# Four neighbouring tokens per partition, with strided transposes and products, in an attention-and-experts kernel

## The reference

```python
x = x + layernorm(attn(layernorm(x), W_in, b_in, W_out, b_out, decay, mix))
x = x + layernorm(ffn(layernorm(x), gate_kernel, w0, w1, wo))
```

## Time and profile before

| | us |
|---|---|
| median of 3 runs (lowest to highest) | 312.19 (311.73 to 312.6) |
| the profiled execution's own time | 312.02 |
| span of its instructions | 310.2 |
| PE busy | 253.0 (82%) |
| PE weight loads busy | 214.3 (69%) |
| DVE / ACT / POOL busy | 201.2 / 186.1 / 176.1 |

### The profile page before, as it was taken

One profiled execution on the slowest core, in us unless ns is written; L12 is line 12 of the kernel. 1 busy time (PEld: TensorE's weight loads), 2 busy tenths in 40 slices (PEclk: granted clock), 3 DMA queues, 4 the chain that ended last, 5 costly groups with the idle time before them and its releaser, 6 DMA issues.

```text
span 310.2 us, 6821 instructions
## 1 busy us (share of the span) xinstructions
PE 253.0 (82%) x1615; PEld 214.3 (69%) x1615; DVE 201.2 (65%) x917; ACT 186.1 (60%) x451; POOL 176.1 (57%) x197
## 2 busy tenths in 40 slices
PE   0558534469999999999999999999999999999300
PEld 0226321357988899888889888898898888878300
DVE  3787979865496568559666846785554336887512
ACT  3575455616576865856675675666666666699601
POOL 7029567267237756774874787777233333568511
PEclk9965555578999999999999999999999999999955
DMA  5999511131121122112112212432322139020056
GB/s 145 207 383 301 150 53 45 43 79 36 46 60 54 42 73 71 44 62 77 56 44 83 66 45 65 111 107 86 88 73 57 51 91 366 17 77 17 0 154 184
DMA packets 27971, 29.56 MB, mean 95 GB/s; under 512 B 4538, under 2 KB 21148, under 8 KB 27936
## 3 DMA queue, kind: packets, MB, share of 16 engines
q1 hardware_dynamic: 22672, 20.04, 22.3%
q0 software_dynamic: 4544, 8.97, 8.9%
q10 hardware_dynamic: 720, 0.13, 0.3%
HBM read 17.53 MB, written 12.05 MB: 95 GB/s over the span
## 4 chain that ended last, share of the span: by engine, by line
PE 70%; DVE 8%; POOL 6%; DMA 5%; ACT 4%; issue 4%; POOLq 0%; SPq 0%; DVEq 0%; ACTq 0%
PE bank L1570 18%; PE bank L1519 10%; PE bank L1520 10%; PE bank L1521 10%; PE bank L1554 9%; POOL expert_rows L411 3%; PE bank L1514 3%; PE bank L1471 2%; PE bank L1444 2%; PE bank L1455 2%; PE bank L1464 1%; DMA sb_early<-pair_rows 1%; POOL pair_rows L422 1%; DMA sb_x<-in_L_attn_x 1%; POOL sb_rs L447 1%
## 5 line engine op out<-in xcount | busy, mean ns | idle before, releaser
L422 POOL DMA_INDIRECT pair_rows<-sb_y_rows,sb_y_pair x71 | 71.2, 1003 | 59.8 <-ACT sb_y_rows L606 40.2
L411 POOL DMA_INDIRECT expert_rows<-sb_row,sb_place x64 | 63.9, 999 | 30.1 <-issue 17.6
L1570 PE MATMUL bank<-sb_w_raw,sb_gatedT 128*128 x568 | 75.0, 275 | 0.0
L1221 DVE TENSOR_TENSOR sb_w_raw<-bank,sb_w_raw 128x512 f32<-128x512 f32 x71 | 48.9, 689 | 31.5 <-PE bank L1521 20.7
L1570 PEld LDWEIGHTS bank<-sb_w_raw,sb_gatedT 128*128 128x128 f32 x568 | 69.0, 192 | 0.1
L1519 PE MATMUL bank<-sb_w_parts,sb_x_hi 128*128 x142 | 62.8, 442 | 0.3 <-DVE sb_x_lo L1214 0.3
L596 ACT ACTIVATE sb_gatedT<-bank 128x512 f32<-128x512 f32 x71 | 42.4, 597 | 32.6 <-PE bank L1554 32.4
L1520 PE MATMUL bank<-sb_w_parts,sb_x_lo 128*128 x142 | 56.7, 399 | 0.0
L1521 PE MATMUL bank<-sb_w_parts,sb_x_hi 128*128 x142 | 56.5, 398 | 0.0
L591 ACT ACTIVATE sb_w_raw<-bank 128x512 f32<-128x512 f32 x71 | 42.5, 599 | 7.4 <-PE bank L1521 6.4
L1554 PE MATMUL bank<-sb_ident,sb_w_raw 128*128 128x128 f32 x284 | 42.9, 273 | 1.1 <-DVE sb_w_raw L1221 1.1
(11 more groups left out here) (177 smaller groups left out, 348.5 us busy)
## 6 DMA issues: line engine op xcount, KB each, us to landing
sb_taken_rows<-expert_rows SPq DMA_DIRECT2D x71, 65.5 KB, 1.8
sb_w_raw<-in_L_ffn_w SPq DMA_DIRECT2D x2, 2048.0 KB, 14.1
sb_w_raw<-pair_rows SPq DMA_DIRECT2D x3, 1024.0 KB, 7.2
out_dram<-sb_x SPq DMA_DIRECT2D x3, 512.0 KB, 6.2
pair_rows<-sb_y_rows,sb_y_pair POOLq DMA_INDIRECT x71, 2.5
sb_x<-in_L_attn_x SPq DMA_DIRECT2D x4, 256.0 KB, 6.4
expert_rows<-sb_row,sb_place POOLq DMA_INDIRECT x64, 2.3
sb_early<-pair_rows SPq DMA_DIRECT2D x2, 512.0 KB, 3.8
```

Source lines behind the costliest of these rows:

```text
L411: pool.indirect_dma_start(expert_rows[:, :], bass.IndirectOffsetOnAxis(ap=place[b % ROWS][:, k, j:j + 1], axis=0), row[b % ROWS][:, j, :], ...
L422: pool.indirect_dma_start(pair_rows[:, :], bass.IndirectOffsetOnAxis(ap=y_pair[group % 2][:, t % PAIRS:t % PAIRS + 1], axis=0), y_rows[slo ...
L1221: dve.tensor_tensor(gated[t % 2][:], p_l2[:], silu[t % 2][:], ALU.mult).then_inc(c["gated"], 1)
L1570: last = pe.matmul(p_y[t % 2][:, 0:D], gatedT[t % 2][:, n * P:(n + 1) * P], wo.rearrange("p o d -> p (o d)"), start=(n == 0), stop=(n == F ...
```

## The change

Partition p holds the tokens 4p to 4p+3 of a batch instead of p, 128+p, 256+p and 384+p. In DRAM these four tokens lie side by side, so a partition's part of a batch is one run of 2 KB instead of four runs of 512 bytes, both where `x` is loaded and where the result is written. Piece j of a batch is now every fourth token, starting at j. To keep the 512 tokens in order along the row for the recurrence, `turn1` writes piece j into every fourth column of the bank, 16 bytes apart, and `times_w_out` takes every fourth column of `states` as its stationary operand. The results of `times_w_out` go to the same places as before, and all later steps keep their code; the numbers 4p + j are now the tokens' own. No instruction is added, removed or moved on any engine: the only things that differ are the shapes of the ten DMAs (line 289 and line 350), the addresses that 32 transposes write, and those that the weight loads of 32 float32 products read, which appear as 64 weight loads and 64 matmuls in the trace.

```diff
-            tokens = x_in.rearrange("b (j p) d -> p (b j) d", p=P)
+            tokens = x_in.rearrange("b (p j) d -> p b (j d)", p=P)
 
             def load_x(n, first, end):
-                sp.dma_start(x[:, first * G:end * G],
-                             tokens[:, first * G:end * G]).then_inc(s_x[n], 16)
+                sp.dma_start(x[:, first * G:end * G].rearrange("p (b j) d -> p b (j d)", j=G),
+                             tokens[:, first:end]).then_inc(s_x[n], 16)
...
-            results = out.rearrange("b (j p) d -> p b j d", p=P)
+            results = out.rearrange("b (p j) d -> p b (j d)", p=P)
...
                 sp.dma_start(results[:, first:end],
-                             x[:, first * G:end * G].rearrange("p (b j) d -> p b j d", j=G)
+                             x[:, first * G:end * G].rearrange("p (b j) d -> p b (j d)", j=G)
                              ).then_inc(s_out, 16)
...
+            def every(columns, j):
+
+                return columns.rearrange("q (p j) -> q j p", j=G)[:, j, :]
+
             def turn1(b):
...
-                    last = pe.transpose(p_first(b)[:, j * P:(j + 1) * P], xn1[b % 2][:, j, :],
+                    last = pe.transpose(every(p_first(b)[:], j), xn1[b % 2][:, j, :],
                                         ident[:])
...
                     last = pe.matmul(p_first(b)[:, j * D:(j + 1) * D],
-                                     states[b % 2][:, j * P:(j + 1) * P], w_outT[:], start=False,
+                                     every(states[b % 2], j), w_outT[:], start=False,
                                      stop=(j == G - 1))
```

## The result

The changed kernel takes 316.69 us, the median of 6 runs (314.44 to 317.88), beside 311.89 us for the kernel before (6 runs): a ratio of 1.0141, 95% interval 1.0113 to 1.0168. By the ratio it is slower by some 4.4 us; the two medians lie 4.8 apart. 315.2 was predicted. One further execution of the kernel before, beside the later experiments, took 449.92 us at a granted clock of 0.577 and is in no ratio. Lines of the changed kernel are 4 higher from `turn1` on: the transposes are L1440, the bias L1455, the products L1459, the tile's first layers L1523 to L1525 and `wo` L1574.

A forecast was written before the change was run, and what follows sets the result against it. PE was taken to bound the loop, with a chain of waits across engines before it and the last batch's after it; +3.10 + 0.27 - 0.2 - 0.2 = +2.97 us gave 315.2 us, with eight in ten from 311.4 to 317.4.

The forecast's parts named there:

- The weight loads, +3.10 in the loop: Batches 4 to 7, products with every-fourth-column weight loads: 32 pairs slower by 97 ns each, ends 0 and 4.35 us.
- The ratio taken from VectorE, 1.87: VectorE's 16-byte-step read against a contiguous one, per element; applied to a PE pair, 111 ns becomes 208 ns.
- The step is free for PE: Rival: weight loads stay at 111 ns a pair, leaving only DMA gains, 311.8 us; chance 0.23, plus 0.10 with full DMA gain.
- Batches 0 to 3: Products ahead of the full PE stretch: batch 2 on the chain costs +0.27 us; batches 0, 1 and 3 are covered, 0.
- a price that grows with the slower clock: Upper end for batch 2's eight pairs at half clock: +1.49 us if the same 1.87 applies there.
- Batch 0's pairs run at 111 ns: Batch 0's products: +0.78 us moves their end to 17.48, but later transposes wait for ACT anyway, so 0.
- The transposes, 0: Transposes writing every fourth PSUM column: no price, four staying at 0.44 us at full clock.
- a time of 0.9 ns for two neighbours: Reason for free transposes: if PSUM takes two neighbouring columns as one write, strided columns every 0.86 ns ask about the same.
- the two rivals in which the transposes pay: Strided PSUM writes cost 1.15 us: both operands pay, 316.3 us, chance 0.12; only PSUM writes pay, 313.0, chance 0.05.
- The last write, -0.2: End of the kernel: the final 262 KB write moves faster in 2 KB runs, gaining between 0 and 0.3 us.
- The first load of `x`, -0.2: Start of the kernel: the first load lands sooner in 2 KB runs, gaining between 0 and 0.7 us on the chain.
- Longer runs slower than short ones no row suggests: DMAs at both ends: nothing in the profile suggests 2 KB runs lose time against 512-byte runs, so no loss was reckoned.

The follow-up runs named there:

- the first four experiments: Kernel before with strided products alone, 1.0121, or strided transposes alone, 1.0000; changed kernel with both PE steps taken back, 1.0053, or 1 KB runs and 8-byte step, 1.0002.
- the next four experiments: In the study's order: kernel before with 2 KB loads, 1.0015, or 2 KB writes, 0.9997; small loads awaited first, with DMAs alone, 1.0052, or 1 KB runs, 1.0057.

## Why the prediction came out as it did

- **The weight loads, +3.10 in the loop: right, a little small.** The loop grew by 3.42, or 107 ns a pair instead of 97. The ratio taken from VectorE, 1.87, was 1.95 here. That it came so near is in part luck: VectorE's own 1.93 ns a column would have made 247 ns a pair, and what the runs show is 1.70 ns a line, hidden up to the 111 ns that a pair takes in any case. The rule that spoke against the change (the Trainium skill, Advanced Engine Details and Errata, SBUF Cachelines: two hits on a line of 16 bytes) agrees with the runs: a pair with one hit on a line takes 217 ns, with two 117, and without a step 111. "The step is free for PE" falls.
- **Batches 0 to 3.** Batch 2 was put at +0.27 and measured +0.12 (2.03 instead of 1.91, and in the chain of the strided products alone 1.83 instead of 1.71), far from the 1.49 of a price that grows with the slower clock. Batches 0, 1 and 3 were put at 0. With the strided products alone POOL's first send of rows starts at 35.38, before at 35.31, and batch 3's averages are done at 66.20, POOL free at 66.25: right, on the thin cover that was reckoned. In the changed kernel batch 0's products do come onto the chain (16.50 to 18.34). The step alone does not put them there: from the start of the bias product to their end they take 1.26 us before and 2.14 with the strided products alone, off the chain, but 2.41 in the changed kernel, where they run as slowly as at half clock (the bias product takes 0.59 us there, and 0.38 in the other two). A contiguous batch 0 that runs so takes 2.30 and is on the chain too, as with the writes alone. "Batch 0's pairs run at 111 ns" held in some executions and not in others, and as the granted clock reads 1.00 over these products, no row tells why.
- **The transposes, 0: right.** Their experiment gives a ratio of 1.0000. The reason given in the prediction is borne out in part: at full clock the bias product, twice as fast a writer, pays up to 0.88 ns a column. But it pays at half clock too, where it writes a column only every 0.90 ns, while the transposes pay nothing at their slower pace either (1.13 us for four with the step, in their experiment at 8.38, and without it). So a time of 0.9 ns for two neighbours is not what decides, and what sets the two kinds of product apart is not shown beyond these rows. "Any non-contiguous AP" (PSUM Cachelines, the same page of the Trainium skill) therefore holds for the bias product and not for these transposes; the two rivals in which the transposes pay fall.
- **The last write, -0.2: wrong.** It lands 0.3 earlier, as reckoned, but the span ends as long after the last add as before, in every profile. The prediction took the landing for the end of the run without a row that said so; what PE's sequencer still does there, no row shows. The Trainium skill's rule (DMA: Bandwidth & Descriptors, the table at its head) makes 512 B enough for line rate; the windows differ from it, 292 GB/s in 512-byte runs and 386 in 2 KB runs. So the term came to nothing for another reason than the rule's.
- **The first load of `x`, -0.2: wrong, and the step that failed.** The prediction let 0.3 us reach the chain, on the ground that at worst the small loads would stay where they are. `x` did come 0.43 earlier. But `W_in`, `W_out` and `b_in` landed 1.0, 0.5 and 1.0 later, and since L1430 already stood 0.31 us ahead of the first transposes, the chain moved over to them: +0.48 at the first product. "Longer runs slower than short ones no row suggests" looked only at the load that got the longer runs and not at the loads beside it. That the runs' length is the reason is likely but not certain: the loads alone had the same front and no delay in their one profile.
- **The sum.** Predicted +3.0, measured +4.4 by the ratio. The loop's +3.4 is shown twice, by the change and by the strided products alone (1.0121, some 3.8 us). The DMAs alone measured +0.53%, some 1.6 us, in place of -0.4: the wrong sign, which the size of the loop's term covers. Multiplied, the two ratios give 1.0175, a little more than the 1.0141 of the change. Of the 1.6 the profiles show some 0.2 to 0.5, as the late first product.
- **What stays open** is the other 1 us or so of the DMAs' price. The profiled loops agree within 0.2 us apart from the strided loads, and the ends within 0.3, so it lies ahead of the loop, where the moment at which the clock rises and falls is worth 1.3 us by itself. That a later front meets a half-speed stretch more often would fit; runs with the loads alone (1.0015) and with the small loads first did not show it, and the latter was no clean test. Executions at like clock point that way: at a mean granted clock of 0.907 or 0.908 the kernel before took 310.19 to 310.51 us beside the first four experiments (four executions), the DMAs alone 311.06 (one) and the change 314.44 and 314.61. That would be 0.7 for the DMAs and 4.2 for the change; but beside the next four experiments the kernel before took 310.22 to 311.61 at this clock (eight), so they are too few to show it.

## What to carry to other kernels

A step in the stationary operand of a product counts, up to 16 bytes, by the 16-byte lines it touches: two float32 to a line are as good as free (117 ns a pair instead of 111), one nearly doubles the pair (217), and where weight loads follow one another without a gap that is paid in full. A step in PE's output depends on the kind of product: the float32 transposes scattered for nothing, and the bias product took nearly twice as long for a column, at full clock and at half. So an operand's step has to be tried with the instruction that will use it. Before a load is sped up at the start of a kernel, look at which small loads run beside it and how little they stand off the chain. And before two executions are compared, look at the stretches in which their clocks differ.

## What the runs showed beside that

- 512-byte runs and 2 KB runs move a lone 256 KB write at 292 and 386 GB/s, and the span ends 3.9 us after the last add with either.
- Small loads are delayed by transfers on another queue that started just before: `b_in`, 0.5 KB, took 5.37 to 5.63 us beside three batches of `x` in 2 KB runs in three executions and 4.5 in a fourth, 4.5 to 5.0 in 512-byte runs, and 3.25 with only one batch beside it.
- A step's price can shrink or grow with the slower clock: 16 bytes in a weight load add 106 ns a pair at full clock and 15 at half, and 16 bytes in the bias product's output add 0.23 us at full clock and 0.43 at half.
- Two executions of one program, within 0.1 us of each other at one product of the first layers (70.59 and 70.68), then part by 1.3 us by the clock of the next four. From 68 to 70 us PE was busy for 0.94 us in the one that kept full speed and for 1.03 in the one that fell to half.
